# Mask groups of 6 destinations by 150 source columns, the first group's edges fetched alone, weights loaded behind them, four logarithm buffers and three PSUM banks for the K/V units in a two-layer graph attention kernel

## The reference

```python
def transformer_conv(x, src, dst, Wq, bq, Wk, bk, Wv, bv, Ws, bs, H, C, concat):
    q, k, v = x @ Wq + bq, x @ Wk + bk, x @ Wv + bv        # each reshaped to (n, H, C)
    alpha = einsum('ehc,ehc->eh', q[dst], k[src]) / sqrt(C)
    p = exp(alpha - segment_max(alpha, dst)[dst])
    denom = segment_sum(p, dst) + 1e-16
    out = segment_sum(p[:, :, None] * v[src], dst) / denom[:, :, None]
    out = out.reshape(n, H * C) if concat else out.mean(axis=1)
    return out + x @ Ws + bs
h = relu(transformer_conv(x, ..., H=4, C=128, concat=True))
y = layernorm(x + transformer_conv(h, ..., H=2, C=128, concat=False))
```

## Time and profile before

| | |
|---|---|
| median of three runs | 1961.21 us (1961.04 to 1963.61) |
| the profiled execution | 1960.0 us, of which the span of the profile is 1957.8 us |
| busy in the span | PE 93%, DVE 79%, ACT 64%, POOL 58% |
| first one-hot instruction of batch 0 (DVE L612) | starts at 30.30 us |
| the eight gathers of groups 1 to 4 (POOL L539) | first starts at 25.17 us, last ends at 36.99 us |
| last one-hot instruction (DVE L612) | ends at 254.78 us |
| last logarithm (ACT L448) | starts at 258.07 us and takes 1.11 us |
| first instruction of layer 1's attention | 264.91 us |

### The profile page before, as it was taken

The page is one execution under the profiler, slowest core; times in us unless marked ns, Lnnn a source line. Parts: engine busy times, 40 slices in busy tenths (PEclk is TensorE's granted clock), DMA queues, the critical chain, the costliest instruction groups (busy, mean ns, idle before and its releaser), DMA issues. The chain is left out here.

```text
span 1957.8 us, 44657 instructions
## 1 busy us (share of the span) xinstructions
PE 1813.7 (93%) x14891; PEld 1350.4 (69%) x14891; DVE 1540.9 (79%) x4569; ACT 1258.3 (64%) x2081; POOL 1142.0 (58%) x1458
## 2 busy tenths in 40 slices
PE   2789969999999999999999999859799999999997
PEld 2555537777777777777777777636467777777776
DVE  5899857888888888888888888522588888888886
ACT  2477647777777777777777777612166666766665
POOL 4000016777767777777677777601267767767775
PEclk9799979999999999999999999979899999999999
DMA  6588766778878877787788878570289999998995
GB/s 143 134 203 204 182 161 129 152 156 157 155 151 157 158 154 152 154 161 154 149 156 160 156 149 148 107 216 1 64 153 170 182 177 167 182 185 174 179 178 108
DMA packets 771276, 302.46 MB, mean 154 GB/s; under 512 B 657124, under 2 KB 751056, under 8 KB 767799
## 3 DMA queue, kind: packets, MB, share of 16 engines
q1 hardware_dynamic: 767143, 295.60, 75.3%
q10 hardware_dynamic: 3266, 2.36, 0.5%
q0 software_dynamic: 640, 1.63, 0.3%
HBM read 93.75 MB, written 48.45 MB: 73 GB/s over the span
## 5 line engine op out<-in xcount | busy, mean ns | idle before, releaser
L1300 DVE CUSTOM_DVE_ANT_0 prob_l<-score_l,mask_l 125x512 f32<-125x512 f32 (+2 forms) x1050 | 644.1, 616 | 215.8 <-PE score_l L1447 214.0
L1447 PE MATMUL score_l<-KT,QT_l 128*128 128x512 f16 (+2 forms) x3150 | 772.1, 355 | 13.0 <-DVE piece_max_l L1300 12.7
L1151 POOL TENSOR_TENSOR prob_parts_l<-prob_l,prob_parts_l 125x512 f16<-125x512 f32 x600 | 721.8, 1233 | 16.0 <-ACT prob_parts_l L1230 16.0
L1221 ACT ACTIVATE prob_l<-prob_l,neg_max_l 125x1024 f32<-125x1024 f32 (+1 forms) x450 | 521.6, 1161 | 4.4 <-DVE neg_max_l L1308 4.3
L1236 ACT CAST probT_l<-transposed_l 128x375 f16<-128x375 f32 x450 | 212.9, 473 | 430.4 <-PE transposed_l L1472 430.4
L1478 PE MATMUL output_l<-V,prob_flipped_l 128*128 128x256 f16 x2400 | 459.5, 272 | 2.9 <-DMA prob_flipped_l<-prob_parts_l 2.9
L1480 PE MATMUL output_l<-V,prob_flipped_l 128*128 128x128 f16 x2400 | 427.4, 219 | 0.0
L1447 PEld LDWEIGHTS score_l<-KT,QT_l 128*128 128x128 f16 x3150 | 282.6, 99 | 144.9 <-DVE piece_max_l L1300 18.8
L1139 POOL CAST QT_l<-q_now_l 128x125 f16<-128x125 f32 x150 | 43.6, 290 | 541.3 <-ACT q_now_l L1208 541.3
L1230 ACT CAST prob_parts_l<-prob_l 125x1024 f16<-125x1024 f32 x300 | 309.5, 1033 | 0.1
L1286 DVE SCALAR_TENSOR_TENSOR mask_l<-mask_l 125x512 f32<-125x512 f32 (+2 forms) x350 | 277.1, 795 | 7.7 <-DMA mask_l<-mask_scratch 7.7
(11 more groups left out here) (170 smaller groups left out, 2023.1 us busy)
## 6 DMA issues: line engine op xcount, KB each, us to landing
mask_scratch<-log SPq DMA_DIRECT2D x79, 448.0 KB
mask_l<-mask_scratch SPq DMA_DIRECT2D x50, 448.0 KB
mask_l<-mask_scratch SPq DMA_DIRECT2D x24, 896.0 KB
mask_l<-mask_scratch SPq DMA_DIRECT2D x24, 471.2 KB
prob_flipped_l<-prob_parts_l SPq DMA_TRANSPOSE x600, 3.3
mask_l<-mask_scratch SPq DMA_DIRECT2D x24, 336.0 KB
hT_scratch<-rowsT_l SPq DMA_DIRECT2D x25, 250.0 KB, 3.7
hT<-hT_scratch SPq DMA_DIRECT2D x6, 1024.0 KB, 14.0
```

Of the source, the lines that this page charges most:

```text
L1151: pool.tensor_tensor(parts[0:TP, 1, a:b], prob[:, h % 2, a:b], parts[0:TP, 0, a:b], ALU.subtract).then_inc(s_flo, 1)
L1221: act.activation(e, e, ACT.Exp, bias=neg_max[:, h % 2:h % 2 + 1], accum_out=total[:, h % 2, c:c + 1]).then_inc(s_exp, 1)
L1300: dve.tensor_tensor_reduce(out=prob[:, h % 2, a:b], in0=score_bank(h, p)[0:TP, 0:b - a], in1=mask[:, parity, a:b], scale=1.0, scalar=-3.0e ...
L1447: last = pe.matmul(score_bank(h, p)[:, 0:b - a], QT[:, h % 2, i, :], KT[:, h, j, a:b], start=n == 0, stop=n == len(products) - 1)
```

## The change

- `WD` = 6, `CB` = 150, so `CA` = 21, `ROWS` = 126 and `WB` = 6: a batch is 6 windows of 6 destinations (36 destinations instead of 40), and `NBAT` is 87. A piece of a destination is 600 bytes, a row of `mask_dram` 12600 bytes (before 12800). A PSUM bank holds 3 windows of 150 columns. PE's one-hot weights are read 128 wide, from rows of 126.
- DVE makes the one-hot rows of two batches with one pair of instructions (`hots`, `PAIR` = 2); `hot` holds 3 such pairs. `LOGS` = 4. The digit is found with two f32 instructions instead of one shift.
- Group 0 has its own chunk comparison (11 instructions of 128 windows), its own `s_chunk` value and its own probe ahead of the others. `first_slots` of groups 1 to 4 stands behind the first `hots`.
- The loads of weights and biases move from ACT's queue to SP's, behind a wait for the two gathers of group 0 (`s_got`).
- V's bias is split by POOL into three bf16 parts, and one bf16 matmul of 96 partitions adds it.
- K and V units alternate from the fifth unit on, use three PSUM banks, and are spread evenly over batches 15 to 85. The constants that place the other steps move.
- The rows of x, the scales and the bias parts live in the room of K (`K_room`), other small tiles in `abs_w`.

```diff
-WD = 5
-CB = 128
+WD = 6
+CB = 150
-WB = 8
+WB = 6
+PAIR = 2
-LARGEST_AFTER, LISTS_AFTER, SCALE_AFTER, ROOT_AT, KV_FROM, CHECK_AFTER = 1, 3, 5, 7, 11, 20
-LISTS_AT = (9, 11, 13, 15)
-KV_EVERY = 5
-LOGS = 3
+LARGEST_AFTER, LISTS_AFTER, BOUNDS_AT, SCALE_AFTER, ROOT_AT, KV_FROM, CHECK_AFTER = 1, 5, 4, 7, 8, 15, 17
+LISTS_AT = (9, 10, 12, 13)
+LOGS = 4
+UNIT_BANKS = 3
+SOON = 4
+LOG_SPLIT = ((0, 112), (112, ROWS))
...
+        order = [("K", n) for n in range(KU - NT + 1)]
+        for t in range(NT):
+            order += [("V", t)] + ([("K", KU - NT + 1 + t)] if t < NT - 1 else [])
+        LAST_AT = NBAT - 2
+        unit_of = {KV_FROM + m * (LAST_AT - KV_FROM) // (UNITS - 1): m for m in range(UNITS)}
...
+                for ends in s_got:
+                    sp.wait_ge(ends[0], 16)
+                sp.dma_start(Wk_sb[:, 0, :], Wk).then_inc(s_wk, 16)
...
-                act.dma_start(Wk_sb[:, 0, :], Wk).then_inc(s_wk, 16)
...
-                for g in range(CG):
-                    dve.tensor_scalar(below[:, g, :], first_dst[:, :], last[:, g:g + 1], None, ALU.is_gt).then_inc(s_below, 1)
...
+                chunks_below(0, 1, 0, CG)
+                chunks_below(1, WG, 0, SOON)
+                first_chunks(0, 1)
+                chunks_below(1, WG, SOON, CG)
+                first_chunks(1, WG)
...
+                def hots(d):
+
+                    windows = range(d * PAIR * WB, min((d + 1) * PAIR, NBAT) * WB)
+                    for i in range(2):
+                        dve.wait_ge(s_rel[i], windows[-1] // C + 1)
+                    wait(dve, s_cnt, PAIR * (d - HOTS + 1))
...
-                        ins = pe.matmul(psum[0:r, :], ones_row[:, 0:r], bv_sb[0:1, :], start=False, stop=True,
+                        ins = pe.matmul(psum[0:r, :], pick[:, 0:r], bias_parts[:, :], start=False, stop=True,
```

More of the change, by code:

```diff
@@ L304, in mask_and_projections @@
         got = [late(10, 3, I32)[:, 0:WG * SLOTS], late(13, 3, I32)[:, 0:WG * SLOTS]]
-        digit = late(16, 3, I32)[:, 0:WG * SLOTS]
+        digit = late(16, 3, F32)[:, 0:WG * SLOTS]
         row_v, col_v = late(19, 3, F32)[:, 0:WG * SLOTS], late(22, 3, F32)[:, 0:WG * SLOTS]
@@ L417, in _ @@
                     sp.wait_ge(s_log, PAIRS + b + 1)
-                    for r0, r1 in ROW_SPLIT:
+                    for r0, r1 in LOG_SPLIT:
                         sp.dma_start(blocks[r0:r1, WB * b:WB * (b + 1), :],
@@ L454, in unit @@
                     act.wait_ge((s_up, s_lowp)[part], m + 1)
-                    if m == KU and part == 0:
+                    kind, t = order[m]
+                    if kind == "V" and part == 0:
                         act.wait_ge(s_pad, 1)
-                    if m < KU:
-                        h = m // NP
+                    if kind == "K":
+                        h = t // NP
+                        if h == H1 - 1:
+                            act.wait_ge(s_parts, 6)
                         ins = act.activation(to[part], psum, ACT.Identity, bias=bk_sb[:, h:h + 1])
@@ L480, in _ @@
                     logarithm(b)
-                    m = unit_at(b)
-                    if m is not None and m < UNITS:
-                        unit(m, 0)
-                    if m is not None and 0 < m <= UNITS:
-                        unit(m - 1, 1)
+                    if b in unit_of:
+                        unit(unit_of[b], 0)
+                    if low_of(b) is not None:
+                        unit(low_of(b), 1)
                 act.wait_ge(s_late, 32)
@@ L624, in _ @@
                 for b in range(NBAT):
-                    batch(b)
+                    if b % PAIR == 0:
+                        hots(b // PAIR)
+                    if b == 0:
+                        first_slots(1, WG)
                     if b == LARGEST_AFTER:
@@ L769, in _ @@
                     if b == KV_FROM:
-                        scales.wait_scaled(pe)
+                        scales.wait_weights(pe)
+                        for kind in range(2):
+                            pe.wait_ge(s_rel[kind], WG)
                         pe.wait_ge(s_minus, 1)
-                        pe.wait_ge(s_const, 8)
-                    m = unit_at(b)
-                    if m is not None and m < UNITS:
-                        unit(m)
-                    if m is not None and 0 < m <= UNITS:
-                        unit_low(m - 1)
+                    if b in unit_of:
+                        unit(unit_of[b])
+                    if low_of(b) is not None:
+                        unit_low(low_of(b))
                 pe.wait_ge(s_many, 1)
@@ L795, in general_batch @@
                         for j in range(BANKS_PER):
-                            pe.matmul(counts(u)[:, j, :], zeros[:, 0:ROWS], zeros[:, :], start=True, stop=False, skip_group_check=True)
+                            pe.matmul(counts(u)[:, j, :], zeros[:, 0:ROWS], zeros[:, 0:PER_BANK * CB], start=True, stop=False, skip_group_check=True)
                         CS = NCH // SLOW
```

213 lines of the change are left out of this document (128 added, 85 removed).

## The result

The changed kernel takes 1939.2 us (median of 4 runs, 1935.94 to 1940.61), the kernel before on the same chip 1961.1 us (4 runs). The ratio is 0.9886, with a 95% interval of 0.9868 to 0.9904: faster by 22 us, where 41 were forecast, and 1.2 us outside the range. The profiled execution took 1935.94 us with a span of 1934.1 us. The last logarithm starts at 234.41 us instead of 258.07; from there to the span's end it is 1699.7 us in both profiled executions. So, in these two, the whole gain, and all that is missing of it, lies in the mask part.

The account below looks back on a forecast made before the run. Only the mask part counted, bound by DVE among K units and PE among V units; terms summed to -40.8 us, last logarithm at about 217 instead of 258.07, giving 1919 us, range 1908 to 1938.

Parts of the forecast that it names:

- The DMA pace: Mask stores: 600-byte packets priced in proportion to bytes, 37 ns each, 1.75 us a batch, just under DVE's 1.795.
- mild store bound: Rival, mask stores: unaligned pieces at 42 ns, 2.0 us a batch, 1926 us; chance 0.21 shared with the early-part rival.
- The full store bound: Rival, mask stores: same mechanism, higher price; 52 ns a packet undoes the gain, 60 ns gives 1986 us; slower: chance 0.06.
- The rule of the Trainium skill: Mask stores: 256-byte transactions must start at multiples of 256, making a 600-byte piece about 1.35 times a 512-byte one.
- The start: Start of the mask part: moved weights and a shorter chunk comparison bring the first one-hot rows to 22.0 us, -8.3 us.
- The wait for the eight gathers: Early mask part: DVE at 38 us waits for gathers of groups 1 to 4, landing about 42; +3.7 us (0 to 6).
- One-hot rows: DVE's mask batches: 3.59 us a pair, 1.795 a batch, 156 us for 87; -22 us (-18 to -25).
- DVE's late waits for PE: Late mask part: DVE's waits for PE to free one-hot rows go, -13.9 us.
- Bounds and bias columns: Mask part: DVE's waits for bounds (3.1) and bias columns (2.8) go, being placed further ahead; -5.9 us (-3 to -6).
- The end: End of the mask part: shorter work between DVE's last one-hot instruction and the last logarithm, -2 us.
- The loss between the engines: Mask batches: PE and ACT at 0.97 hold DVE up by 0.1 us a batch, +7 us (0 to 15).
- The attention at nothing: Attention, after the mask part: costed at nothing, with the same mask columns loaded and PE work covering the loads.

Follow-up runs that it names:

- lists later: LISTS_AFTER raised from 5 to 8, against the kernel with pieces of 608 bytes: 1917.38 us, ratio 0.9779 to the kernel before the change.

## Why the prediction was wrong

The direction was right, and only the mask part counted. DVE was to set its pace; in the change the stores do, and DVE does only once the stores are out of the way. The time was off by 20 us. In order of the prediction's steps:

- **The DMA pace, the step that failed.** "in proportion 37 ns each, 756 x 37 / 16 = 1.75 us. So DVE at 1.795 is just the slowest." Measured: 41 ns spaced and 1.94 us a batch, so that the stores are the slowest, not DVE. The cause is where the pieces begin in DRAM: at multiples of 32 bytes the kernel takes 16.5 us less, although the pieces are longer. "In proportion" was wrong for aligned pieces too, to the other side: 608 bytes take 35.8 ns, where it gives 37.4. The rival of the mild store bound named both the mechanism and its price (42 ns, 2.0 us a batch), and the gain of 22 us lies in its class of 20 to 36. The price was assumed and not worked out, so that its closeness is partly luck, and it holds only back to back (34.9 ns with half of the stores). The rival got 0.21, together with another case, for want of a row with an unaligned piece; the DMA share of 0.92 at 2.25 us a batch, which left a margin of 0.05 us a batch, deserved more weight. Its 1926 us was too low as it let the stores begin at 77 us with 15 batches done, while 12 were done at 80.
- **The full store bound** is real too, though not for this change, and its break-even price was worked out about right: "52 ns a packet" was to undo the whole gain. At 51.3 ns the last logarithm starts at 269.05 us, 11 us later than before, since the early part is also later than the rival had it. A base 8 bytes further is enough for that.
- **The rule of the Trainium skill**, "DMA: Bandwidth & Descriptors", section "How a descriptor splits into AXI transactions" (a transaction must start at a multiple of 256 bytes; the page's words are of reads), warned in the right direction, but these stores do not follow it. By its beats alone a piece of 600 bytes comes to 1.44 times one of 512 (an estimate from that page, 23 beats in the mean against 16; the prediction has 1.35), and measured are 41.1 / 31.5 = 1.30 back to back and 1.11 with half of the stores. Pieces of 608 bytes miss that boundary seven times in eight and take 1.14 times as long, hardly more than by their length, and a source moved by 8 bytes costs nothing. What the runs with a moved destination resemble is a line of "Collectives: The Full Stack", section "Rules for kernel authors": buffers aligned to 32 bytes avoid a read-modify-write. The page says it of collectives' buffers, and no run here shows the reads themselves.
- **The start**, -8.3 us: measured -7.5. The probe landed at 13.41 (forecast 13.4), the edges at 18.62 (18.0), and the steps behind them took 0.2 us more than taken. The landing was right for a partly wrong reason: the 8.43 us wait for the probe was put down to the weights, but with the weights back in front it is 5.73 us.
- **The wait for the eight gathers**, +3.7 us: measured 7.8. They landed 5.7 us after the last issue had ended, since the first stores (from 33 us on) share the DMA engines with them, which the forecast of 42 us did not count. With half of the stores it is 3.8 us and with the moved destination 7.5, and DVE's waits, in this order, are

```profile
44.39 0.79 DVE L676 TENSOR_SCALAR V<-V 128x1024 f32<-128x1024 int32 x1 [5.86 <-DMA V<-in_src,start_i]
48.16 0.69 DVE L674 TENSOR_SCALAR V<-V 128x1024 f32<-128x1024 int32 x1 [9.57 <-DMA V<-in_src,start_i]
```

The eight issues on POOL took 12.5 us, of which 11.8 were forecast. The step's range ended at 6.
- **One-hot rows**, -22 us: a pair takes 3.59 us, as taken (104.43 to 108.02).
- **DVE's late waits for PE**, -13.9 us: right. In the kernel with 608 bytes there are none; in the change 6.9 us are left, which come from the stores through ACT and PE, as they are gone with half of the stores. Putting back the f32 bias alone brings 7.8 us of waits back and moves the last logarithm by 14.1 us, so it is that matmul, and not the order of units, on which the late waits stood. That 14.1 is near to 13.9 may be chance: only 7.8 of it are waits of DVE for PE. In the changed kernel the bias matmul (L811) takes 0.38 us in the mean; below 0.45 was forecast.
- **Bounds and bias columns**, -5.9 us: both waits are gone. In their place came two that had no term: DVE for PE's transposes, 1.2 and 1.9 us, because lists at batches 9 and 10 (and 12 and 13) lie between the same two pairs of one-hot rows; and 1.6 us in one-hot rows that run beside POOL's bias chain.
- **The end**, -2 us: with pieces of 608 bytes -1.1 (2.2 us from DVE's last rows to the last logarithm instead of 3.3), in the change +5.6.
- **The loss between the engines**, +7 us: it was not there. The prediction had PE and ACT at 0.97 of DVE's time; with 608 bytes both are at 0.94, for PE above all because a V unit takes 1.34 us instead of 1.52 (139.45 to 140.79 us in that trace). The row behind PE's price was also read too high: 1502.41 - 1502.36 is 50 ns, not 55. This error of +7 us hid part of the others.
- **The attention at nothing**: right within what can be told. The first profiled executions agree to 0.1 us; the second one of the same kernel is 3.3 us longer there.

Put together with these values, the sum for the kernel with 608 bytes is -7.5 + 7.0 + 0.7 - 22 + 0.9 (wider columns) - 13.9 - 5.9 + 3.2 + 1.6 - 1.1 = -37.0, a last logarithm at 221.1 us; it starts at 220.19. Most of these values were read from the same traces, so that the sum says that no large term is missing, and no more. The unaligned stores add 14.2 to 220.19 (234.41).

What stays open: why back-to-back stores slow down when their pieces are unaligned, and the finest alignment that is enough. The stretch behind the last logarithm varies from 1699.7 to 1704.9 us among these kernels, with no pattern that the edits explain; 3.3 us of it were seen between two executions of one kernel. Part of it goes with TensorE's granted clock in the 20 us behind the last logarithm: 0.54 in the second execution of the change and with the moved source, 0.64 in the first; 500 us behind the last logarithm the two are 2.5 and 2.0 us later than the first. Before the change too the granted clock is below 1.0 in more places than between 40 and 80 us: 0.92 from 80 to 100, 0.83 from 100 to 120 and 0.60 from 260 to 280 us.

## What to carry to other kernels

When a new tile shape changes the size of a DMA piece, check its alignment in DRAM as well as its bytes: 2 columns more, which no reader of the result needed, were worth 16.5 us, and a base 8 bytes off took more than the whole change gave. That shows once the stores run back to back. Where the slowest engine leaves the DMA engines a few per cent, a price that "goes by bytes" is the term to bound first, and a rival that names a mechanism and a pace deserves more than a remainder of the chances. A wait of the engine that will be the bound costs its length even 50 us before it becomes the bound, as in the kernel with lists later.

## What the runs showed of the hardware

- With the store queue nearly or wholly full, a store from SBUF to DRAM in pieces takes 31.5 ns a piece for 512 bytes, 35.8 for 608 and 36.7 for 640 when each starts at a multiple of 32 bytes; 41 for 600 bytes that start at multiples of 8 (34.9 when the queue is busy for 0.465 of the time), and 51.3 for 608 bytes that all start 8 bytes past a multiple of 32. An offset of 8 bytes on the SBUF side changes nothing (35.7). These are prices of a DMA engine with all 16 at work, and in bytes the queue moved 252 GB/s with pieces of 608 bytes, 227 with 600 and 184 with the moved destination. With the 600-byte pieces the DMA share read 1.04 to 1.09 in the profiled execution, so that there the spacing of packets is the safer price.
- DVE's f16 comparison of 128x3600 took 2.99 us instead of 2.03, and one of 128x3024 2.01 instead of 1.73, while POOL worked on the bias parts. In the kernel with lists later POOL's chain runs 8 us earlier, and so do the long comparisons (2.01 us at 65.61, 3.00 at 67.54). The timeline of POOL in the changed kernel, beside the rows of DVE at 73.85 and 75.78:

```profile
73.00 0.61 POOL L612 CAST KT<-KT 96x512 bf16<-96x512 f32 x1
73.67 0.60 POOL L614 COPY bias_parts<-KT 32x512 bf16<-32x512 bf16 x1
74.35 2.53 POOL L615 TENSOR_TENSOR bias_parts<-KT 32x512 bf16<-32x512 f32 x1
```

- An indirect gather's issue on POOL takes 0.94 or 0.95 us mostly, and 1.3 to 2.0 in some cases. The stores are not what sets this: with half of them the long ones take the same 2.00, 1.64, 1.34 and 1.64 us. It goes with DVE's one-hot instructions. The last of the eight issues takes 0.94 or 0.95 us in the eight kernels with lists at their first place, where DVE stands and waits, and 1.33 or 1.34 in the five with lists later, where DVE makes one-hot rows. The change first, then lists later:

```profile
40.03 0.94 POOL L576 DMA_INDIRECT V<-in_src,start_i  x1 [0.30 <-issue]
39.56 1.34 POOL L576 DMA_INDIRECT V<-in_src,start_i  x1 [0.30 <-issue]
```

Before the change two issues took 1.94 and 1.95 us, both beside one-hot instructions; one beside the first of these took 0.95, so that not every overlap costs.
